# Gated attention and routed experts on one core: rows turned before they are normalised, routing begun inside the last attention chunk, the first expert unit put together in PSUM, and 16 products of the output weights whose result nobody reads

## The reference

```
x = x + tanh(g_xattn) * attention(layernorm(x), ctx; Wq, Wkv, Wout)   # 16 heads of 32, causal softmax
h = layernorm(x)
route = sigmoid(h @ router_w)                 # 8 experts
e = argmax(route); p = max(route)             # one expert per token
y = (silu(h @ gate_w[e]) * (h @ up_w[e])) @ down_w[e]
x = x + tanh(g_ffn) * p * y
```

## Time and profile before

| what | value |
| --- | --- |
| time, median of 3 runs | 536.86 us |
| time of the profiled execution | 538.37 us |
| its span in the trace | 536.7 us |
| mean granted TensorE clock | 0.95 |
| PE busy | 475.5 us (89%) |
| DVE busy | 383.3 us (71%) |
| ACT busy | 306.6 us (57%) |
| POOL busy | 170.6 us (32%) |
| DMA | 77.32 MB, mean 144 GB/s |

### The profile page before, as it was taken

The page is one execution under the profiler, slowest core; times in us unless marked ns, Lnnn a source line. Parts: engine busy times, 40 slices in busy tenths (PEclk is TensorE's granted clock), DMA queues, the critical chain, the costliest instruction groups (busy, mean ns, idle before and its releaser), DMA issues.

```text
span 536.7 us, 11376 instructions
## 1 busy us (share of the span) xinstructions
PE 475.5 (89%) x3659; PEld 400.6 (75%) x3659; DVE 383.3 (71%) x809; ACT 306.6 (57%) x871; POOL 170.6 (32%) x210
## 2 busy tenths in 40 slices
PE   0978999899989999763899999999999999999890
PEld 0966796689668767553789888888888888888770
DVE  3674767967886477886377778777787777877750
ACT  0557757773876478411356575575666656656630
POOL 3315225533653445253231122132212212320121
PEclk9995999899999999975799999999999999999996
DMA  8600220340041023742376867778767778667620
GB/s 191 192 3 2 63 47 2 111 139 16 10 141 34 1 71 101 253 115 40 79 225 205 268 208 217 227 204 273 213 213 237 214 252 247 209 221 237 191 63 30
DMA packets 58911, 77.32 MB, mean 144 GB/s; under 512 B 5074, under 2 KB 40506, under 8 KB 58880
## 3 DMA queue, kind: packets, MB, share of 16 engines
q1 hardware_dynamic: 53728, 66.90, 41.6%
q0 software_dynamic: 5152, 10.03, 6.3%
HBM read 67.76 MB, written 10.34 MB: 146 GB/s over the span
## 4 chain that ended last, share of the span: by engine, by line
PE 30%; DVE 24%; issue 18%; ACT 11%; DMA 10%; POOL 3%; SPq 1%; DVEq 1%; ACTq 1%; POOLq 0%
DMA staging<-in_L_ffn_gate_w 7%; ACT wq_hi L664 4%; ACT gu_hi L664 4%; DVE gu_lo L893 4%; PE bank L1517 3%; PE bank L1410 3%; PE bank L1412 3%; PE bank L1411 3%; DVE qT L1371 3%; DVE v L1364 2%; DMA staging<-in_L_xattn_Wq 2%; DVE v L1356 2%; DVE xn L1386 2%; DVE wq_lo L893 2%; PE gate_banks L1504 2%
## 5 line engine op out<-in xcount | busy, mean ns | idle before, releaser
L893 DVE TENSOR_TENSOR gu_lo<-staging,gu_hi 128x1024 fp32r<-128x1024 f32 x64 | 78.3, 1224 | 18.4 <-ACT gu_hi L664 17.9
L1796 PE MATMUL gate_banks<-x_hl,gu_hi 128*128 128x448 f32 x256 | 85.9, 386 | 3.7 <-issue 1.3
L1796 PE MATMUL up_banks<-x_hl,gu_hi 128*128 128x448 f32 x256 | 83.3, 377 | 0.0
L493 POOL TENSOR_TENSOR pn<-pr,inv 100x400 f32<-100x400 f32 x64 | 54.4, 853 | 62.9 <-DVE inv L1064 62.7
L664 ACT ACTIVATE gu_hi<-staging 128x1024 fp32r<-128x1024 f32 x64 | 67.1, 1051 | 5.5 <-DMA staging<-in_L_ffn_gate_w 5.3
L1798 PE MATMUL gate_banks<-x_hl,gu_lo 128*128 128x224 f32 x256 | 69.2, 270 | 0.0
L1798 PE MATMUL up_banks<-x_hl,gu_lo 128*128 128x224 f32 x256 | 68.4, 267 | 0.0
L1796 PEld LDWEIGHTS gate_banks<-x_hl,gu_hi 128*128 128x128 f32 x256 | 49.2, 192 | 10.5 <-issue 2.5
L664 ACT ACTIVATE wkv_hi<-qT 128x448 fp32r<-128x448 f32 x32 | 18.5, 578 | 67.3 <-DVE qT L1371 67.3
L1410 PE MATMUL bank<-wq_hi,wkv_hi 128*112 128x512 f32 x128 | 50.9, 398 | 4.3 <-DVE xn L1386 3.4
L715 ACT ACTIVATE pr<-gate_banks,nmx 100x100 f32<-100x100 f32 x128 | 42.2, 354 | 17.7 <-DVE nmx L1058 17.5
(11 more groups left out here) (229 smaller groups left out, 1121.8 us busy)
## 6 DMA issues: line engine op xcount, KB each, us to landing
staging<-in_L_ffn_gate_w SPq DMA_DIRECT2D x32, 512.0 KB, 5.3
staging<-in_L_ffn_up_w SPq DMA_DIRECT2D x32, 512.0 KB, 7.4
staging<-in_L_ffn_down_w SPq DMA_DIRECT2D x32, 512.0 KB, 4.0
x_rows<-x SPq DMA_DIRECT2D x8, 800.0 KB
xt<-in_x SPq DMA_DIRECT2D x4, 800.0 KB
xr<-in_x SPq DMA_DIRECT2D x16, 200.0 KB
staging<-in_L_xattn_Wq SPq DMA_DIRECT2D x1, 1024.0 KB, 11.1
x<-in_L_xattn_Wout SPq DMA_DIRECT2D x1, 1024.0 KB, 9.2
```

What stands on the lines that cost most here:

```text
L493: nc.gpsimd.tensor_tensor(pn[0:S, n % DEEP], pr[0:S, n % 2], inv[0:S, n % HP].unsqueeze(2).to_broadcast([S, HP, S]), ALU.mult).then_inc(pr ...
L893: return nc.vector.tensor_tensor(dst, src, hi.bitcast(F32), ALU.subtract)
L1796: nc.tensor.matmul(pair[:, m, 0:2 * CAP], gu_hi[:, s, w, k, r], x_hl[:, :, k, 0:CAP], start=k == 0, stop=False, skip_group_check=True)
```

## The change

It touches the last chunk, the passage and the first unit; the loop over chunks and the loop over units stay.

- PE turns the rows of `x1` without normalising them (`turn_row`); the mean is taken out of the router instead (`router_mean`, `centre_router`: `router_c` is the mean minus the router), and the reciprocal root goes into the exponential's scale (`exp_rows`). The root of the last chunk is one POOL power (`root_rows`) in place of the Newton steps.
- The last chunk's parts are three batches and one. The first three are turned and routed inside `attend_last`. The orders of all engines in `attend_last` are rewritten; four weight blocks are loaded before the last `scores` and three are split inside it; the chunk before's tokens are scattered between the POOL steps of the heads.
- The first unit's input is summed up in PSUM (`first_b`): `gather_late` multiplies the normalised rows of each batch with a 0/1 matrix of 100 by 224 (`in_unit`), `turn_early` adds the rows of earlier chunks, which two indirect DMAs gathered. Both write the transposed layout, so `find`, the gather of unit 0, `turn_tokens(0)` and `split_tokens(0)` go; `split_first` takes their place.
- The unit list: six of its 16 DVE steps (`unit_names`) move into `attend_last`, ten (`unit_counts`) follow `split_first`. Their bodies are unchanged.
- `keep_warm(n)` multiplies `wo_hi` with itself, 128 by 512, n times into a bank that nobody reads: 2, 2, 2, 4 and 6 times.
- Two constants more are written by POOL at the start.

```diff
+            for w in range(3):
+                load_weights(0, 0, 0, w)
+            load_weights(0, 0, 1, 0)
+            load_residual(NCH - 1, 2)
             sp.wait_ge(s_ready.sem, s_ready.after(NCH, 0))
-            for j in range(2):
-                load_step(0, 0, j)
+            for w in range(1, 3):
+                load_weights(0, 0, 1, w)
+            load_residual(NCH - 1, 3)
+            sp.wait_ge(tok_scattered.sem, tok_scattered.after(NCH - 2, 16 * CB))
+            sp.dma_start(idx_now[0:TR], token_table[0:CAP, :].rearrange("(p t) o -> p (t o)", p=TR)).then_inc(early_loaded, 16)
+            sp.dma_start(x1_rows[bass.ds((NCH - 2) * CT, CT), H:XW].rearrange("(i s) d -> s i d", s=S), whole.scale[0:S]
+                         ).then_inc(scale_stored, 16)
             store_x1(NCH - 1)
             store_x2(NCH - 1)
-            sp.wait_ge(xg_loaded.sem, xg_loaded.after(0, 16 * TT))
...
+            def root_rows(part):
+                b = part.batches
+                pool.wait_ge(last_var_ready, part.number + 1)
+                nc.gpsimd.tensor_tensor(norm2.rstd[0:S, b], norm2.var[0:S, b], minus_half[0:S, b], ALU.pow).then_inc(last_root_done, 1)
+            def normalise_late(c):
+                pool.wait_ge(ln2_ready.sem, ln2_ready.after(c, 2))
+                pool.sem_inc(wait_passed, 1)
+                normalise(x2, x1, norm2, CB - 1).then_inc(x2_done.sem, 1)
...
+            def gather_early(c):
+                pool.wait_ge(early_cleared, 1)
+                pool.wait_ge(x2_stored.sem, x2_stored.after(c, 0))
+                pool.wait_ge(early_loaded, 16)
+                pool.sem_inc(wait_passed, 1)
+                for t in range(TT):
+                    nc.gpsimd.indirect_dma_start(early[0:TR, t, :], None, x2_rows[0:T - CT, :],
+                                                 bass.IndirectOffsetOnAxis(ap=idx_now[0:TR, t:t + 1], axis=0),
+                                                 bounds_check=T - CT - 1, oob_is_err=False).then_inc(early_gathered, 16)
...
+                clear_early(c)
                 scale_probs(c, 12)
                 scale_probs(c, 13)
+                scatter_token(c - 1, whole, 0)
+                scatter_token(c - 1, whole, 1)
                 scale_probs(c, 14)
                 scale_probs(c, 15)
+                scatter_token(c - 1, whole, 2)
+                scatter_token(c - 1, whole, 3)
+                root_rows(last_parts[0])
+                gather_early(c)
                 normalise_rows(c, 0)
                 normalise_rows(c, 1)
+                normalise_rows(c, 2)
+                root_rows(last_parts[1])
+                normalise_late(c)
...
-            gather_tokens(0)
-            pool.wait_ge(early_loaded, 16)
-            for part in last_parts:
-                scatter_tokens(NCH - 1, part)
-            store_scale(NCH - 1, last_parts[1])
+            scatter_tokens(NCH - 1, last_parts[0])
             pool.wait_ge(rows_known, 1)
             nc.gpsimd.indirect_dma_start(unit_table, bass.IndirectOffsetOnAxis(ap=u_slot[0:MORE, :], axis=0),
                                          unit_row[0:MORE, :], None, bounds_check=UNITS_MAX - 1,
                                          oob_is_err=False).then_inc(units_scattered, 16)
+            scatter_tokens(NCH - 1, last_parts[1])
             pool.wait_ge(units_scattered, 16)
             nc.gpsimd.dma_start(units[:], unit_table.rearrange("(a u) w -> a (u w)", a=1)).then_inc(units_loaded, 16)
-            pool.wait_ge(tok_scattered.sem, tok_scattered.after(NCH, 0))
+            store_scale(NCH - 1, last_parts[1])
+            pool.wait_ge(x1_stored.sem, x1_stored.after(NCH, 0))
+            pool.wait_ge(x2_stored.sem, x2_stored.after(NCH, 0))
+            pool.wait_ge(tok_scattered.sem, tok_scattered.after(NCH, -16))
+            pool.wait_ge(scale_stored, 16)
...
                 exponentials(c, 12)
                 exponentials(c, 13)
+                split(0, 0, 0)
+                split_output(c, 2)
                 exponentials(c, 14)
                 exponentials(c, 15)
+                keep_normed(c, 0, row_b)
+                split(0, 0, 1)
+                keep_normed(c, 1, row_b)
+                split(0, 1, 1)
                 split_output(c, 3)
+                keep_normed(c, 2, row_b)
+                exp_rows(c, last_parts[0])
+                split(0, 1, 0)
+                keep_normed(c, 3, row_b)
+                exp_rows(c, last_parts[1])
+                split_first(0)
+                split_first(1)
+            def exp_rows(c, part):
+                act.wait_ge(last_root_done, part.number + 1)
+                act.wait_ge(logits_ready.sem, logits_ready.after(c, part.stop))
+                for i in range(part.first, part.stop):
+                    ins = nc.scalar.activation(ex[0:S, i], part.ex_b[i], ACT.Exp, scale=norm2.rstd[0:S, i:i + 1])
+                ins.then_inc(ex_done.sem, 1)
+            def split_first(h):
+                act.wait_ge(gT_ready.sem, gT_ready.after(0, h + 1))
+                copy(x_hi[:, 2 * h:2 * h + 2, 0:CAP], first_b[h][:, 0:2 * CAP].rearrange("p (k s) -> p k s", k=2)
...
+            def choose_rows(c, part):
+                if part.number == 0:
+                    chain.add(nc.vector.tensor_copy(toks[1][0:S], tok_f[0:S]))
+                for k in range(7):
+                    settled(choose, c, part, k)
+                if part.number:
+                    chain.add(nc.vector.tensor_tensor(late_first[0:S], cand[0:S, CB - 1, 0:1], best[0:S, CB - 1:CB], ALU.is_equal))
+                choose(c, part, 7)
...
+            def in_first_unit(c):
+                chain.settle()
+                dve.wait_ge(o_ready.sem, o_ready.after(c, CB))
+                for i in range(CB - 1):
+                    nc.vector.tensor_scalar(in_unit[0:S, i].rearrange("p t q -> p (t q)"),
+                                            slot_of[0:S].rearrange("p t q -> p (t q)"), slot_f[0:S, i:i + 1], None,
+                                            ALU.is_equal).then_inc(in_unit_done, 1)
+            def late_var(c):
+                i = CB - 1
...
+                link(nc.vector.tensor_tensor(var, var, tmp, ALU.add))
+                dve.sem_inc(last_var_ready, 1)
...
+            def late_in_first_unit(c):
+                part = last_parts[1]
+                dve.wait_ge(rank_ready.sem, rank_ready.after(c, 2))
+                link(nc.vector.tensor_tensor(late_slot[0:S], part.rank[:, 0, 0:1], next_slot[0:S, 0:1], ALU.add))
+                nc.vector.tensor_scalar(in_unit[0:S, CB - 1].rearrange("p t q -> p (t q)"), slot_of[0:S].rearrange("p t q -> p (t q)"),
+                                        late_slot[0:S, 0:1], late_first[0:S, 0:1], ALU.is_equal, ALU.mult).then_inc(in_unit_done, 1)
...
+            def split_first(h):
+                dve.wait_ge(g_hi_done.sem, g_hi_done.after(0, h + 1))
+                lo_part(x_lo[:, 2 * h:2 * h + 2, 0:CAP], first_b[h][:, 0:2 * CAP].rearrange("p (k s) -> p k s", k=2),
+                        x_hi[:, 2 * h:2 * h + 2, 0:CAP]).then_inc(g_lo_done.sem, 1)
...
+                first_rows_var(c)
                 low_output(c, 3)
+                first_rows_shift(c)
+                choose_rows(c, last_parts[0])
                 split(0, 0, 0)
                 residual(c, 3)
                 rows_stats(c, 3)
+                place_rows(c, last_parts[0], 0, 3)
+                in_first_unit(c)
+                late_var(c)
+                split(0, 0, 1)
+                late_shift(c)
+                place_rows(c, last_parts[0], 3, PLACE_STEPS)
+                choose_rows(c, last_parts[1])
+                late_in_first_unit(c)
+                place_rows(c, last_parts[1], 0, PLACE_STEPS)
+                split_first(0)
+                split_first(1)
+                unit_counts()
+                split(0, 1, 0)
+                split(0, 1, 1)
...
+            def turn_row(c, i):
+                pe.wait_ge(x1_done.sem, x1_done.after(c, i + 1))
+                if i:
+                    pe.wait_ge(x2T_copied.sem, x2T_copied.after(c, i))
+                else:
+                    pe.wait_ge(exp_done.sem, exp_done.after(c, NT - HP + 1))
+                for k in range(KC):
+                    ins = nc.tensor.transpose(row_b[:, k * S:(k + 1) * S], x1[0:S, i, k * P:(k + 1) * P], ident[0:S, 0:S])
+                ins.then_inc(x2T_ready.sem, 1)
+            def route_row(c, i):
+                pe.wait_ge(x2T_copied.sem, x2T_copied.after(c, i + 1))
+                part = last_parts[0] if i < last_parts[0].stop else last_parts[1]
+                if i == 0:
+                    pe.wait_ge(router_centred, 1)
+                    pe.wait_ge(exp_done.sem, exp_done.after(c, NT - HP + 2))
+                elif i == CB - 1:
+                    pe.wait_ge(exp_done.sem, exp_done.after(c, NT))
+                for k in range(KC):
+                    ins = nc.tensor.matmul(part.ex_b[i], x2T[:, k, i * S:(i + 1) * S], router_c[:, k, :],
```

(113 more changed lines are left out.)

279 lines of the change are left out of this document (145 added, 134 removed).

## The result

| | before | after |
| --- | --- | --- |
| median of 4 runs | 536.15 us | 528.75 us (528.53 to 528.79) |
| profiled execution | 538.37 us | 528.79 us |
| its span | 536.7 us | 527.3 us |
| end of the last `project` (T) | 228.78 | 228.23 |
| first gate product starts | 255.72 (T + 26.9) | 243.76 (T + 15.5) |

The ratio is 0.9856, 95% interval 0.9825 to 0.9888: faster by 7.4 us in the medians and 9.4 us between the two profiled spans. The profiled execution of before is 2.2 us above its own median, that of after is at it, hence the difference between 7.4 and 9.4. Of the 9.4, T gives 0.55, the passage 11.15, and the units take back 2.3.

The account below looks back on a forecast made before the run. PE bounds attention and units, with a passage of waits between; the second gate product comes 11.5 us earlier, less 2.75 for half clock, 8.8 gained: 529.6 profiled, 528 median, range 523.5 to 535.

Parts of the forecast that it names:

- the list's way: From the known unit list through POOL and DRAM to the second gate product: scatter, load, reading and wake, 8.3 us.
- the cold stretch: Units after the second gate product starts: the next 5.5 us run at half clock and cost 2.75 us.
- T unchanged: End of the last project stays at 228.78 us, walked as 228.1, with ends -1.5 and +3.
- First gate product at T + 14.1: Passage after attention: gate_up(0, 0) starts near 242.9 us instead of 255.72.
- at full clock if the fillers do their work: PE from T to the first gate product: unread products keep the clock up, longest stop under 1 us.
- clock at half ahead of the first gate product: Sign against the forecast: half clock in the windows before that product, where 1.00 was expected from T on.
- rival 2: Early gather lands 2.5 us late, PE stops before gather_late(0) and the clock falls there: 533.3 us, chance 0.18.
- List known at T + 16.4: DVE's ten unit_counts steps start at T + 14.1, take 2.1 us, and the unit list is then known.
- The list, not unit 0's products, holds the second gate product: First product ends at T + 19.3; PE waits 5.4 us for the list, second starts at T + 24.7.
- The clock falls in the long stop: PE's 5.4 us stop before the second gate product drops the clock to half, costing 2.75 us.
- rival 1: The clock stays up over the 5.4 us stop, so 11.5 us are gained: 525.4 us, chance 0.17.
- Rivals 3 and 4: Chunk 2's routing delays the last chunk: 538, chance 0.08; something other than PE holds the list: 535.5, chance 0.07.

Follow-up runs that it names:

- a7: The changed kernel with three more unread products ahead of the last row's turn; 526.77 us, ratio 0.980.
- a8: The changed kernel with a7's three unread products, twelve in PE's long stop, and DVE's splits held until a POOL fill behind the list scatter's issue; 524.09 us, ratio 0.977.
- a4: The changed kernel with eight more unread products ahead of the first gate product, so unit 0 starts later; 527.27 us, ratio 0.983.
- a3: The changed kernel with the six unit_names steps put back from the last chunk to just ahead of unit_counts; 528.84 us, ratio 0.986.
- b2: The kernel before with 14 unread products where PE waited for the rows of unit 0; 537.89 us, ratio 1.001.
- a2: The changed kernel with 16 more unread products in PE's stop after the first gate and up product; 526.96 us, ratio 0.983.
- a6: The changed kernel with a5's waiting splits and 14 unread products in PE's stop after the first gate and up product; 526.07 us, ratio 0.980.
- b1: The kernel before with the unit list's scatter issued ahead of the four token scatters and the scale store; 534.12 us, ratio 0.994.
- a1: The changed kernel with all 16 unread products left out; 529.12 us, ratio 0.987.
- a5: The changed kernel with DVE's two weight splits of step 1 waiting for POOL's signal after the list scatter; 528.29 us, ratio 0.983.

## Why the prediction was right, point by point
528.0 was forecast and 528.75 measured; for the profiled execution 529.6 and 528.79. The mechanism held: a long stop ahead of the first product gone, the list as the next bound, half clock behind its stop. That the number came so near is partly luck. The gathers were 1.4 late, and against it stood T (0.55 early), the list's ten steps and its settling (0.3 less), the list's way (0.7 less) and the cold stretch (0.45 less); and the 1.5 us by which the median was put below the profiled execution were 0.04. Its steps:

- **T unchanged.** Right: 228.78 became 228.23, and 227.5 to 229.1 in the variants; the order of before had T from 225.5 to 229.4 in its four profiled executions, so the 0.55 says nothing. `scores(3)` ended at 208.7 (209.4 forecast), the rest of the chunk took 19.6 (18.7). Two readings in the walk were off: the row of 1.58 for sixteen router instructions is two batches, so one batch is 0.79 and not 0.4 (0.79 measured), which puts 1.2 us more ahead of T; and PE's idle time between `scores(3)` and T was 3.2, not 3.7.
- **First gate product at T + 14.1.** 15.5. The step that failed is "at full clock if the fillers do their work": the clock fell at 232.3 and the three gathers took 6.11 instead of 4.70, which is all of the 1.4. At full clock a7 has 14.04. The count of stops was right (the longest 0.73); that a stop under 1 us would spare the clock was not. The prediction had named clock at half ahead of the first gate product as a sign that it is wrong, and for this step the sign came. The row that it went by was also misread a little: in the earlier trace rows the clock falls at 234.2 and not 234.4, 2.2 us into the stop.
- **Sizes beside it.** `gather_late` 4.70 / 3 = 1.57 (1.6 forecast). The Trainium skill's four passes for true FP32 ("FP8 and Floating Point Precision", TensorE Precision Notes) give an estimate of 1.5 for it; the trace agrees within 5%. The early gather began at T - 0.4 (T + 1), so rival 2 had no ground. The power took 0.90 and 1.67, not 0.3, and its worst case 0.8 was too low; `hot` came at T + 10.4 (8.7 to 9.5) behind it, still no later than PE's way to `rank` with the fall. In a8, at full clock, PE does wait 0.39 for it.
- **List known at T + 16.4.** 17.5, by the same 1.4 less 0.3. Behind it 7.6 instead of 8.3.
- **The list, not unit 0's products, holds the second gate product.** Shown by a4 (product moved, mark not), a3 (list moved, mark moved), b2 (in the kernel before as well, by a stop of 5.10).
- **The clock falls in the long stop.** Right: 4.25 us of it (5.4 forecast), and the cold stretch costs 2.3 in the trace (2.75). a2 and a6 take it away; rival 1 is out. a2 showed what hid behind it: unit 1's rows, 0.37 us. POOL's next gather began 2.2 after the second gate product (4.3 forecast), but its index load waited 6.2 us, with SP's three weight blocks (issued from 253.8) ahead of it; before, it took 2.4, and in a8, where it was issued 0.6 ahead of those blocks, 2.4 too.
- **Rivals 3 and 4.** No round of 5 us opened in attention; POOL was ready for the list 5 us ahead.

## What to carry to other kernels
When a stage waits for two things that come within 1.5 us of each other, an edit to either one alone shows little (b1 0.6%, b2 nothing), so look for the one that will hold afterwards: here the way of a small table through POOL and DRAM. Unread products are worth what they do to the clock at the place where they stand: fourteen or sixteen in the 4 us stop shortened the stretch behind it by 1.5 to 2.6 us, three more ahead of the last row's turn brought both marks 1.5 forward, and the sixteen spread over the passage brought nothing. A two-input DVE step beside a POOL instruction that issues a DMA can double its length; to move it away helps only if no other such instruction of the same chain then stands beside it (a8).

## What the hardware showed that I had not expected
- The granted clock can fall while PE is fully busy, 2.6 us after the end of a stop of only 0.73 (at 232.3 in the profile after), and comes back inside the same run of gathers (at 235.8).
- A POOL instruction that issues an indirect DMA takes 0.93 to 1.0 alone and 1.84 to 2.25 beside a VectorE split of 128x1024 (the Trainium skill's "GPSIMD Engine Reference", 8. Key points, names the shared interface for DVE steps with two inputs; the trace agrees, and shows that issuing a DMA suffers too). Which of the two starts first matters: the first early gather took 2.04 to 2.25 in the profiles of after, its repeat, a1, a2, a5 and a8, where the split began ahead of it or at most 0.07 us later, and 1.10 in a3, a4, a6 and a7, where the split began 0.10 to 0.29 later. A POOL power took 0.90 for three columns with no split beside it and 1.66 for one column beside one; one column alone is in no run.
- A semaphore given by POOL's sequencer after an instruction in the program came 0.24 us before that instruction began to run; a small POOL instruction's own signal kept the order.
- The attention stage had a cold stretch of 14 us near 40 to 53 and one of 3 us at 105 in the kernel before, of 10 us and one of 3 us at 152 in b1, and of 7 us in a7. Among the runs of one kernel the time goes with the mean granted clock (the kernel before: 534.05 us at 0.958, 540.95 us at 0.944). Which cold stretch makes the difference is not shown: a7's shorter one left T at 227.98, where a8 with 14 us had 227.64.
